# Skip term and gate product as single VectorE steps, with Q ahead of V and a new order of all steps, in an attention and Mamba-2 kernel on one core

## The chip, the cores and the metric

The kernel runs on one core of one Trainium2 chip. The metric is the device time of one execution in microseconds; where several executions were made, their median. A core has five engines that run side by side and wait for each other by semaphores: PE (TensorE, matmuls into PSUM), DVE (VectorE), ACT (ScalarE), POOL (GpSimd) and SP (SyncE, which here only issues DMAs).

## What is computed

The input x is 4 images of 128 channels and 32 x 32 points, so 1024 tokens of 128 channels for each of 4 batches. A block of attention is followed by a Mamba-2 block. Cut to what matters:

```python
# attention, per batch
h = group_norm(x, 8 groups) * gn_w + gn_b
q, k, v = split(h @ qkv_w.T + qkv_b)
x = (softmax(q @ k.T / sqrt(128)) @ v) @ proj_w.T + proj_b + x

# Mamba-2, per batch, on tokens of x
u = layernorm(x) * norm_g + norm_b
z, xBC, dt = split(u @ in_w.T)
dt = softplus(dt + dt_bias)
xs, Bm, Cm = split(silu(conv4(xBC) + conv_b))        # causal, 4 taps, one filter per channel
state_t = state_{t-1} * exp(dt_t * A) + dt_t * xs_t * Bm_t
y = state_t . Cm_t + Dp * xs                          # Dp * xs is the skip term
y = y * silu(z)                                       # the gate product
y = y * rsqrt(mean(y*y) + eps) * rms_w
out = y @ out_w.T
pooled = mean(out over tokens)
attn = sigmoid(relu(pooled @ se1_w.T + se1_b) @ se2_w.T + se2_b)
result = x + out * attn
```

## The kernel before

**Batches and steps.** The four batches are called a, b, c and d. The work of all of them is cut into named steps, and one table, `ORDER` (lines 59 to 130), lists every step once: the name of its kind, a number, the batch, and for some the PSUM bank (`@0` to `@2`). Each engine walks through the whole table and emits the steps that are its own, so the table alone sets the order of the instructions on every engine; semaphore waits hold each step until what it needs is there. Attention of one batch is laid over the Mamba block of the batch before it.

**Attention.** `h` (float32), `h_hi` and `h_lo` are the normalised input and its split in two halves of lower precision. `Q0`, `Q1` multiply them with the product of the key and query weights, ACT makes `q_hi` and DVE `q_lo`. `V0`, `V1` are the values (line 1093). For each of 8 tiles of 128 queries there are two halves of keys: `S` (the scores, three matmuls of 512 columns each, line 1103), `max` on DVE over both halves (line 879), two `exp` on ACT (line 597), two transposes `T` on PE (line 1111), their copies `pT` on ACT (line 603) and two `PV` on PE (line 1120). So `S0` and `S1` are the first tile and `S14`, `S15` the last. Then DVE scales and adds (`inv`, `res`) and takes the statistics of the layer norm (`stats`, `ln_ve`).

**Mamba, in halves of 512 tokens.** `UT` transposes the normalised tokens, `InX`, `InBC`, `InZ` and `Dt` project them. `conv_x` are four taps: the first on ACT, the others on DVE (line 918). `conv_bc` has its taps on ACT (`term`, line 636) and POOL (line 508). `sp0` to `sp17` are the softplus on DVE. `L0` to `L7` are matmuls that spread decays to the chunks of 128 tokens, and `l` the DVE scans over them (line 969); `m` (line 981) multiplies them with `G`. `to_end` (DVE), `xend` (POOL), `U` (PE), `st` (a scan on DVE, line 989), `stc` (ACT) and `Yo` (PE) carry the state from chunk to chunk; `Y` is the part inside a chunk.

**What the change touches.** `yo` on DVE (line 998) brings in the state's part. The skip term is two steps on POOL: `dx` (lines 524 and 526) is `xs * Dp`, held in the buffer of `sq`, and `yo_dx` (line 532) adds it. `y` on DVE (line 1005) adds the chunk's part. The gate product is made of `zt`, the tanh of z/2, and `zv`, z/2, both on ACT, and two POOL steps per half: one multiplies, one adds (line 501). `g` (line 536 on POOL, line 1014 on DVE for the last half of batch d) applies it. `sq`, `Ss`, `ms`, `y_pow` give the inverse root in `y_rstd`; `Out` is the output projection, `o` (line 707) its scaled copy, `Pl` (line 1241) the sums over tokens, `pl`, `SeA`, `hdn`, `SeB`, `tha` the small network behind them, `gated` (line 1022) and `fin` the last two operations, and a DMA carries each half out.

**The start.** The attention weights come by three DMAs on one semaphore, `attn_w_in`: `wqkv`, `wpT` and `ob_row`. `kq_mm` and `vp_mm` on PE wait for all three. `gn_stats0`, `gn_mm10`, `gn_dev0`, `gn_mm20`, `gn_ve0`, `gn_pow0`, `gn_aff0` are the group norm's steps of batch a, and `warm` are matmuls whose result is not used.

## Time and profile before

| what | value |
|---|---|
| median of 3 runs | 313.5 us (313.08 to 313.89) |
| the profiled execution | 313.5 us |
| its span, first to last instruction | 311.8 us |
| mean granted TensorE clock | 0.977 |
| PE busy | 277.1 us, 89% |
| DVE busy | 238.7 us, 77% |
| ACT busy | 205.6 us, 66% |
| POOL busy | 139.5 us, 45% |

The span is the time of the profiled execution without 1.7 us around it. The profile says for each engine how long it was busy and, for each stretch of idle time, whose work ended it. A wait costs time only where the waiting engine is the one that sets the end of its stretch. Matmuls are pipelined and their rows overlap, so the sum of their durations is more than the busy time.

### The profile page before, as it was taken

How to read it: one execution, taken by the hardware profiler on the slowest of the kernel's cores; microseconds unless marked ns; L12 is line 12 of the kernel's file. 1: busy time of each engine (PE TensorE's matmuls, PEld its weight loads, DVE VectorE, ACT ScalarE, POOL GpSimd, SP SyncE). 2: the span in 40 equal slices, each digit the busy share in tenths (PEclk: the TensorE clock that was granted, in tenths of full speed). 3: DMA queues.
4: the chain of work that ended last, by engine and by line, in shares of the span. 5: the costliest groups of instructions: out<-in, count | busy, mean ns of one | idle time of the engine just before them, and what ended most of it. 6: DMA issues, size and time to landing. Idle time of an engine off the chain costs nothing.

```text
span 311.8 us, 6225 instructions
## 1 busy us (share of the span) xinstructions
PE 277.1 (89%) x2016; PEld 231.5 (74%) x2016; DVE 238.7 (77%) x520; ACT 205.6 (66%) x401; POOL 139.5 (45%) x146
## 2 busy tenths in 40 slices
PE   2689999999999999999999999997999997869762
PEld 1677898887678988878897888786789875637661
DVE  5657555596989759677997999798886898988823
ACT  1134578887796875898759748867857856684230
POOL 7110102521139401853482512990627285775980
PEclk9999999999999999999999999999999999995995
DMA  6900000000000000000000000100000000000003
GB/s 182 408 29 1 2 0 3 0 2 0 2 0 2 3 2 0 0 2 3 1 2 0 2 0 2 38 34 0 2 0 2 2 2 1 0 2 0 37 34 135
DMA packets 3786, 7.32 MB, mean 23 GB/s; under 512 B 651, under 2 KB 1580, under 8 KB 3756
## 3 DMA queue, kind: packets, MB, share of 16 engines
q1 hardware_dynamic: 3212, 6.72, 5.8%
q8 instruction: 17, 0.28, 0.4%
q10 hardware_dynamic: 544, 0.21, 0.2%
q14 instruction: 13, 0.11, 0.1%
HBM read 4.83 MB, written 2.10 MB: 22 GB/s over the span
## 4 chain that ended last, share of the span: by engine, by line
PE 56%; DVE 18%; issue 10%; POOL 7%; ACT 6%; DMA 2%; DVEq 0%; SPq 0%; ACTq 0%; POOLq 0%
PE mamba L1039 18%; PE scores L1039 14%; PE attn_out L1039 14%; PE turn L1111 6%; DVE neg_max L879 3%; PE turn L1039 2%; DVE L L969 2%; DMA ob_row<-in_proj_b 2%; POOL gate L501 2%; ACT probs L597 1%; DVE pre L918 1%; POOL ln_rstd L490 1%; DVE x_all L1022 1%; POOL y_rstd L541 1%; DVE ln_raw L894 1%
## 5 line engine op out<-in xcount | busy, mean ns | idle before, releaser
L1039 PE MATMUL attn_out<-values,pT 128*128 128x129 f32 x512 | 67.3, 276 | 2.3 <-DVE res L890 1.8
L1039 PEld LDWEIGHTS attn_out<-values,pT 128*128 128x128 f32 x512 | 62.7, 191 | 8.4 <-issue 7.1
L597 ACT ACTIVATE probs<-scores,neg_max 128x512 f32<-128x512 f32 x64 | 41.8, 683 | 14.7 <-DVE neg_max L879 13.8
L879 DVE TENSOR_REDUCE neg_max<-scores 128x1 f32<-128x1024 f32 x32 | 39.0, 1218 | 15.4 <-PE scores L1039 15.4
L603 ACT ACTIVATE pT<-turn 128x512 f32<-128x512 f32 x64 | 37.7, 593 | 13.7 <-PE turn L1111 12.1
L969 DVE TENSOR_TENSOR_SCAN L<-mamba,ident 128x512 f32<-128x512 f32 x32 | 38.6, 1215 | 4.8 <-PE mamba L1039 4.6
L1111 PE MATMUL turn<-ident,probs 128*128 128x128 f32 x256 | 38.2, 274 | 0.0
L1111 PEld LDWEIGHTS turn<-ident,probs 128*128 128x128 f32 x256 | 30.7, 143 | 5.1 <-issue 2.0
L508 POOL TENSOR_TENSOR pre<-pre,th 128x512 f32<-128x512 f32 x16 | 21.7, 1353 | 27.0 <-issue 13.0
L1039 PE MATMUL scores<-h_hi,q_hi 128*128 128x512 f32 x64 | 29.3, 457 | 3.6 <-ACT probs L597 2.3
L1039 PE MATMUL mamba<-u,winC 128*128 128x512 f32 x48 | 25.1, 607 | 0.8 <-DVE L L981 0.5
L1039 PE MATMUL scores<-h_hi,q_lo 128*128 128x512 f32 x64 | 25.3, 395 | 0.0
L1039 PE MATMUL scores<-h_lo,q_hi 128*128 128x512 f32 x64 | 25.1, 393 | 0.0
L515 POOL TENSOR_TENSOR xend<-xdt,to_end 128x512 f32<-128x512 f32 x8 | 9.5, 1192 | 34.7 <-DVE to_end L976 17.1
L501 POOL TENSOR_TENSOR gate<-gate,zv 128x512 f32<-128x512 f32 x16 | 20.9, 1306 | 8.9 <-ACT gate L654 8.6
L490 POOL TENSOR_TENSOR ln_rstd<-ln_var,neg_half 128x4 f32<-128x4 f32 x8 | 9.4, 1175 | 33.6 <-DVE ln_var L901 33.5
L981 DVE TENSOR_TENSOR L<-L,mamba 128x512 f32<-128x512 f32 x32 | 20.9, 676 | 2.3 <-PE mamba L1039 2.2
L918 DVE SCALAR_TENSOR_TENSOR pre<-raw,vec,pre 128x512 f32<-128x512 f32 x24 | 19.1, 794 | 1.1 <-ACT pre L629 1.0
L1039 PEld LDWEIGHTS scores<-h_hi,q_hi 128*128 128x128 f32 x64 | 12.1, 189 | 8.6 <-issue 5.8
L1039 PE MATMUL mamba<-dA_head,pick_chunk 128*128 128x512 f32 x32 | 15.9, 512 | 0.7 <-DVE y L1005 0.3
L610 ACT ACTIVATE u_tok<-res,ln_rstd 128x128 f32<-128x128 f32 x32 | 10.2, 394 | 6.9 <-POOL ln_rstd L490 6.9
L697 ACT ACTIVATE stateT<-scanned 128x512 f32<-128x512 f32 x8 | 9.1, 1144 | 8.5 <-DVE scanned L989 8.5
(198 smaller groups left out, 626.2 us busy)
## 6 DMA issues: line engine op xcount, KB each, us to landing
res<-in_x_tok SPq DMA_DIRECT2D x4, 512.0 KB, 7.8
out<-res SPq DMA_DIRECT2D x8, 256.0 KB, 2.0
x_all<-in_x SPq DMA_DIRECT2D x3, 512.0 KB, 8.3
x_all<-in_x SPq DMA_DIRECT2D x2, 256.0 KB, 3.2
winT<-in_in_wT SPq DMA_DIRECT2D x1, 194.0 KB, 6.7
wqkv<-in_qkv_w ACTq DMA_DIRECT2D x1, 192.0 KB, 3.6
wpT<-in_proj_wT SPq DMA_DIRECT2D x1, 64.0 KB, 3.6
ob_row<-in_proj_b SPq DMA_DIRECT2D x1, 64.0 KB, 5.9
```

Of the source, the lines that this page charges most:

```text
L490: pool.tensor_tensor(ln_rstd[:, four], ln_var[:, four], neg_half[:, four], ALU.pow).then_inc(ln_rstd_ready.sem, 1)
L501: pool.tensor_tensor(gate[:, half], gate[:, half], zv[:, half], ALU.add if part else ALU.mult).then_inc(gate_ready.sem, 1)
L508: pool.tensor_tensor(pre[:, 1, half_of(n)], pre[:, 1, half_of(n)], term(b, n, j), ALU.add).then_inc(tap["bc"].sem, 1)
L597: act.activation(probs[:, i % 2, half_of(h)], scores[:, half_of(h)], ACT.Exp, bias=neg_max[:, i:i + 1]).then_inc(exp_done.sem, 1)
L603: act.activation(pT[:, i % 2, QUAD * h:QUAD * (h + 1), :], bank[:, :].rearrange("p (a b) -> p a b", a=QUAD), ACT.Copy).then_inc(pT_ready.s ...
L610: last = act.activation(u_tok[:, i, :], res[:, b, i, :], ACT.Copy, scale=ln_rstd[:, i:i + 1])
L879: V.tensor_reduce(neg_max[:, n:n + 1], scores[:, :], AX.X, ALU.max, negate=True).then_inc(max_ready.sem, 1)
L918: V.scalar_tensor_tensor(pre[:, 0, half_of(n)], raw[:, 0, n * HALF + j:(n + 1) * HALF + j], vec[:, CONV_X + j:CONV_X + j + 1], pre[:, 0, h ...
L969: V.tensor_tensor_scan(L[:, HEADS * n:HEADS * (n + 1), :].rearrange("p a b -> p (a b)"), bank[:, :], ident4[:, :, :].rearrange("p a b -> p ...
L981: V.tensor_tensor(M[:, HEADS * n:HEADS * (n + 1), :], L[:, HEADS * n:HEADS * (n + 1), :], bank[:, tile(c)].unsqueeze(1).broadcast_to([P, H ...
L1039: return T.matmul(o, w, v, start=start, stop=stop)
L1111: last = T.transpose(bank[:, tile(c)], probs[:, i % 2, tile(QUAD * h + c)], ident[:, :])
```

## The change

- **Skip term.** `dx` is gone. `yo_dx` is one DVE instruction, `(xs * Dp) + yo`; for the first half a second, small one writes the first chunk of 128 tokens.
- **Gate product.** One DVE instruction per half, `(gate + 1) * zv`, in place of the two on POOL.
- **Convolution, first half of batch d alone.** Its three later x taps go from DVE to ACT (`term_x`) and POOL.
- **Start.** The weights have two semaphores, so `kq_mm` waits for `wqkv` alone. `gn_mm10` stands ahead of `kq_mm`, `V0` and `V1` behind `Q0` and `Q1`, `vp_ev` behind `Q0`, and there are 5 warm matmuls in place of 10.
- **Last sums, batch d.** `Out` is copied unscaled (`o_raw`), and `Pl` multiplies the unscaled copy with `y_rstd` as its moving column, so `Pl` no longer waits for `o`. `o` scales from that copy into the buffer of `gated`.
- **Order.** The table is written anew throughout. Of the 32 tiles of scores (8 in each batch) 18 now have their two score steps next to each other on PE, in place of 15; the others have one or more steps between them.

```diff
 ORDER = """
-gn_stats0 warm3 kq_mm gn_mm10 vp_mm gn_dev0 kq_ev gn_mm20 gn_ve0 vp_ev gn_pow0 gn_aff0 h0a h_hi0a V0a@0 h_hi1a h_lo0a
-h1a warm10 Q0a h_lo1a q_hi0a win_s Q1a v0a V1a@1 gn_bs3 v1a q_hi1a q_lo0a q_lo1a S0a gn_bs1 S1a win_mm max0a xob0a
...
+gn_stats0 warm3 gn_mm10 kq_mm gn_dev0 gn_mm20 kq_ev vp_mm gn_ve0 gn_pow0 gn_aff0 h0a h_hi0a h_hi1a h_lo0a h1a warm5
+Q0a vp_ev h_lo1a q_hi0a Q1a q_lo0a V0a@1 win_s q_hi1a q_lo1a S0a S1a gn_bs3 win_mm max0a V1a@0 gn_bs2 exp0a v0a S2a
...
@@ signals and helpers
-        dx = sq
-        vec_in, attn_w_in = signal("vec_in"), signal("attn_w_in")
+        vec_in, qkv_w_in, proj_w_in = signal("vec_in"), signal("qkv_w_in"), signal("proj_w_in")
+        def x_on_pool(b, n):
+            return (b, n) == (BATCH - 1, 0)
+        def term_x(n, j):
+            return th[:, 0, half_of(n)] if j % 2 else x_all[:, half_of(n)]
@@ POOL
-                elif kind == "gate":
...
-                    pool.tensor_tensor(gate[:, half], gate[:, half], zv[:, half], ALU.add if part else ALU.mult
-                                       ).then_inc(gate_ready.sem, 1)
+                elif kind == "conv_x" and n % TAPS and x_on_pool(b, n // TAPS):
...
+                    pool.tensor_tensor(pre[:, 0, half_of(n)], pre[:, 0, half_of(n)], term_x(n, j), ALU.add
+                                       ).then_inc(tap_x_pool.sem, 1)
-                elif kind == "dx":
...
-                        pool.tensor_scalar(yo[:, 0:P], xs[:, 0:P], vec[:, DP:DP + 1], 0.0, ALU.mult, ALU.add)
...
-                    pool.tensor_scalar(dx[:, part], xs[:, part], vec[:, DP:DP + 1], 0.0, ALU.mult, ALU.add
-                                       ).then_inc(dx_ready.sem, 1)
-                elif kind == "yo_dx":
...
-                    pool.tensor_tensor(yo[:, part], yo[:, part], dx[:, part], ALU.add).then_inc(yo_dx_ready.sem, 1)
@@ ACT
+                elif kind == "term_x":
...
+                    act.activation(term_x(n, j), raw[:, 0, n * HALF + j:(n + 1) * HALF + j], ACT.Copy,
+                                   scale=vec[:, CONV_X + j:CONV_X + j + 1]).then_inc(term_x_ready.sem, 1)
+                elif kind == "o_raw":
+
+                    bank = take(act, b, "Out", n)
+                    act.activation(o_tok[:, QUAD * n:QUAD * (n + 1), :], bank[:, :].rearrange("p (i c) -> p i c", i=QUAD),
+                                   ACT.Copy).then_inc(o_raw_ready.sem, 1)
@@ DVE
+                elif kind == "yo_dx":
+
+                    part = slice(P, HALF) if n == 0 else half
+                    if n == 0:
+                        V.tensor_scalar(yo[:, 0:P], xs[:, 0:P], vec[:, DP:DP + 1], None, ALU.mult)
+                    wait(dve, yo_ready, b, n + 1)
+                    V.scalar_tensor_tensor(yo[:, part], xs[:, part], vec[:, DP:DP + 1], yo[:, part], ALU.mult, ALU.add
+                                           ).then_inc(yo_dx_ready.sem, 1)
+                elif kind == "gate":
+
+                    wait(dve, zt_ready, b, n + 1)
+                    wait(dve, zv_ready, b, n + 1)
+                    V.scalar_tensor_tensor(gate[:, half], gate[:, half], 1.0, zv[:, half], ALU.add, ALU.mult
+                                           ).then_inc(gate_ready.sem, 1)
@@ PE
-                        wait(pe, o_ready, b, n + 1)
+                        wait(pe, o_raw_ready, 0, n + 1)
+                        wait(pe, y_rstd_ready, b, n + 1)
                         tiles = [o_tok[:, QUAD * n + k, :] for k in range(QUAD)]
                     for k, t in enumerate(tiles):
-                        last = mm(bank[:, 0:1], t, ones[:, 0:1], k == 0, k == len(tiles) - 1)
+                        factor = ones[:, 0:1] if b < BATCH - 1 else y_rstd[:, QUAD * n + k:QUAD * n + k + 1]
+                        last = mm(bank[:, 0:1], t, factor, k == 0, k == len(tiles) - 1)
```

Three places show the new order on an engine. In the rows, `scores<-ident` are the warm matmuls, `key_query` belongs to Q, `value_proj` to V, `turn<-ident,probs` is T and `attn_out` is PV.

The first is the start on PE, from its first matmul. Before:

```order
L1039 MATMUL scores<-ident 128x128 x3
L1039 MATMUL turn<-wqkv 128x128
L1039 MATMUL turn<-vec,wqkv 128x1
L1039 MATMUL mamba<-gn_mv,group_avg 128x1
L1039 MATMUL turn<-wpT,wqkv 128x128
L1039 MATMUL turn<-wpT,vec 128x128
L1039 MATMUL mamba<-gn_dev,group_avg 128x1
L1039 MATMUL turn<-value_proj,h 128x128 x4
L1039 MATMUL scores<-ident 128x128 x10
L1039 MATMUL scores<-h_hi,key_query_hi 128x512
```

And now:

```order
L1075 MATMUL scores<-ident 128x128 x3
L1075 MATMUL mamba<-gn_mv,group_avg 128x1
L1075 MATMUL turn<-wqkv 128x128
L1075 MATMUL turn<-vec,wqkv 128x1
L1075 MATMUL mamba<-gn_dev,group_avg 128x1
L1075 MATMUL turn<-wpT,wqkv 128x128
L1075 MATMUL turn<-wpT,vec 128x128
L1075 MATMUL scores<-ident 128x128 x5
L1075 MATMUL scores<-h_hi,key_query_hi 128x512
L1075 MATMUL scores<-h_lo,key_query_hi 128x512
L1075 MATMUL scores<-h_hi,key_query_lo 128x512
L1075 MATMUL scores<-h_hi,key_query_hi 128x512
```

The group norm's first matmul has moved ahead of the one that waits for weights, and V0 from ahead of Q to behind it.

The second is PE from the very last scores of batch d (S15) on. Here `xend,BT` is U, `pick_chunk` is L, `ident,xs` is XsT, `BC,stateT` is Yo and `u_tok` is UT. Before:

```order
L1039 MATMUL scores<-h_hi,q_lo 128x512
L1039 MATMUL attn_out<-values,pT 128x129 x4
L1039 MATMUL mamba<-winC,u 128x128 x4
L1111 MATMUL turn<-ident,probs 128x128 x8
L1039 MATMUL mamba<-u,winC 128x512
L1039 MATMUL mamba<-ones,o_sum 128x1 x2
```

And now:

```order
L1075 MATMUL scores<-h_hi,q_lo 128x512
L1148 MATMUL turn<-ident,probs 128x128 x4
L1075 MATMUL mamba<-xend,BT 128x128 x4
L1075 MATMUL attn_out<-values,pT 128x129 x4
L1075 MATMUL mamba<-dA_head,pick_chunk 128x512
L1207 MATMUL mamba<-ident,xs 128x128 x4
L1075 MATMUL attn_out<-values,pT 128x129 x8
L1075 MATMUL mamba<-BC,stateT 128x128 x3
L1075 MATMUL mamba<-dA_head,pick_chunk 128x512
L1148 MATMUL turn<-ident,probs 128x128 x4
L1075 MATMUL attn_out<-values,pT 128x129 x8
L1148 MATMUL turn<-ident,probs 128x128 x4
```

U0, L6, Yo0 and L7 of batch c stood ahead of the last scores and now stand behind them, and nine PV steps of batch d are left there in place of seven.

The third is DVE near its end, from `to_end1` of batch d on. Before:

```order
L976 COPY to_end<-L 128x16
L1022 SCALAR_TENSOR_TENSOR x_all<-th_att,y 128x512
L998 TENSOR_TENSOR th<-mamba,decay_in 128x384
L981 TENSOR_TENSOR L<-L,mamba 128x512 x2
L989 SCALAR_TENSOR_TENSOR scanned<-chunk_decay,mamba 128x512
L1005 TENSOR_TENSOR y<-mamba,th 128x512
L981 TENSOR_TENSOR L<-L,mamba 128x512 x2
L998 TENSOR_TENSOR th<-mamba,decay_in 128x512
L1022 SCALAR_TENSOR_TENSOR x_all<-th_att,y 128x512
L1005 TENSOR_TENSOR y<-mamba,th 128x512
```

And now:

```order
L997 COPY to_end<-L 128x16
L1053 COPY pooled<-mamba 128x1
L1033 SCALAR_TENSOR_TENSOR gate<-gate,zv 128x512
L1002 TENSOR_TENSOR L<-L,mamba 128x512 x3
L1010 SCALAR_TENSOR_TENSOR scanned<-chunk_decay,mamba 128x512
L1058 SCALAR_TENSOR_TENSOR x_all<-th_att,y 128x512
L1002 TENSOR_TENSOR L<-L,mamba 128x512
L1040 TENSOR_TENSOR y<-mamba,th 128x512
L1058 SCALAR_TENSOR_TENSOR x_all<-th_att,y 128x512
L1019 TENSOR_TENSOR th<-mamba,decay_in 128x512
L1027 SCALAR_TENSOR_TENSOR th<-xs,vec,th 128x512
L1040 TENSOR_TENSOR y<-mamba,th 128x512
```

The last gate product and the last skip term have come onto DVE, and the first half's `yo` has moved ahead of this stretch.

## Rows read from the trace of the kernel before

**Rows 1.** Busy time by stage: stretch, length, busy time of each engine, PE clock, DMA.

```profile
0.00:21.10 21.10, 12.23 (x61) 11.39 (x61) 12.56 (x39) 4.25 (x7) 7.34 (x31) 1.00 0.64 229
21.10:237.00 215.90, 207.80 (x1503) 175.34 (x1504) 169.15 (x372) 162.00 (x311) 86.35 (x76) 1.00 0.01 4
237.00:255.20 18.20, 17.86 (x156) 15.15 (x154) 17.04 (x38) 13.02 (x29) 9.75 (x9) 1.00 0.01 3
255.20:288.00 32.80, 26.23 (x160) 18.50 (x158) 28.76 (x53) 20.95 (x44) 21.53 (x20) 0.90 0.00 1
288.00:297.90 9.90, 6.60 (x96) 5.50 (x96) 7.47 (x13) 1.93 (x3) 8.28 (x7) 1.00 0.08 29
297.90:311.80 13.90, 6.41 (x46) 5.56 (x46) 3.76 (x10) 3.44 (x11) 6.25 (x5) 0.73 0.24 94
```

**Rows 2.** Timeline of PE, start to second tile: start, length, instruction, [idle before].

```profile
4.82 1.65 PE L1039 MATMUL scores<-ident 128*128 128x128 f32 x6 [4.82 <-POOL sp_coef L459]
8.11 0.80 PE L1039 MATMUL turn<-wqkv 128*128 128x128 f32 x2 [1.64 <-DMA ob_row<-in_proj_b]
...
8.98 0.57 PE L1039 MATMUL mamba<-gn_mv,group_avg 128*128 128x1 f32 x2
...
13.31 2.04 PE L1039 MATMUL turn<-value_proj,h 128*128 128x128 f32 x8 [2.34 <-DVE h L866]
15.14 3.56 PE L1039 MATMUL scores<-ident 128*128 128x128 f32 x20
18.46 0.48 PE L1039 MATMUL scores<-h_hi,key_query_hi 128*128 128x512 f32 x1
...
19.93 1.05 PE L1039 MATMUL turn<-value_proj,h 128*128 128x128 f32 x8
21.06 0.47 PE L1039 MATMUL scores<-h_hi,q_hi 128*128 128x512 f32 x1
...
26.19 0.47 PE L1039 MATMUL scores<-h_hi,q_hi 128*128 128x512 f32 x1 [0.69 <-ACT probs L597]
```

**Rows 3.** Timeline of DVE, the same stretch, columns as above.

```profile
6.19 0.21 DVE L798 BATCH_NORM_AGGREGATE gn_mv<-gn_raw 128x2 f32<-128x12 f32 x1
...
12.62 0.55 DVE L866 TENSOR_SCALAR h<-x_all,gn_scale,gn_bias 128x512 f32<-128x512 f32 x1
13.53 0.69 DVE L871 TENSOR_TENSOR h_lo<-h,h_hi 128x512 fp32r<-128x512 f32 x1 [0.37 <-ACT h_hi L580]
```

**Rows 4.** The page's part 6, DMA issues: size and time to landing.

```profile
wqkv<-in_qkv_w ACTq DMA_DIRECT2D x1, 192.0 KB, 3.6
```

**Rows 5.** Groups of instructions by shape: busy time, mean ns, idle time before them.

```profile
L969 DVE TENSOR_TENSOR_SCAN L<-mamba,ident 128x512 f32<-128x512 f32 x32 | 38.6, 1215 | 4.8 <-PE mamba L1039 4.6
...
L981 DVE TENSOR_TENSOR L<-L,mamba 128x512 f32<-128x512 f32 x32 | 20.9, 676 | 2.3 <-PE mamba L1039 2.2
L501 POOL TENSOR_TENSOR gate<-gate,zv 128x512 f32<-128x512 f32 x16 | 20.9, 1306 | 8.9 <-ACT gate L654 8.6
L918 DVE SCALAR_TENSOR_TENSOR pre<-raw,vec,pre 128x512 f32<-128x512 f32 x24 | 19.1, 794 | 1.1 <-ACT pre L629 1.0
...
L532 POOL TENSOR_TENSOR th<-th,sq 128x512 f32<-128x512 f32 x4 | 5.4, 1356 | 0.7 <-DVE th L998 0.6
```

**Rows 6.** Line 1022 on DVE: durations ns, least, median, most.

```profile
L1022 DVE SCALAR_TENSOR_TENSOR x_all<-th_att,y x8: 681/688/1759, 186.6 to 307.4; 128x512 f32<-128x512 f32 x8
```

**Rows 7.** Waits of DVE from 237 to 298: us in total, times, longest.

```profile
DVE y L1005 <- POOL th L532: 1.2, 1, 1.2
```

**Rows 8.** Timeline of POOL near the end, columns as in rows 2.

```profile
295.62 1.58 POOL L532 TENSOR_TENSOR th<-th,sq 128x512 f32<-128x512 f32 x1 [0.62 <-DVE th L998]
...
300.88 1.02 POOL L541 TENSOR_TENSOR y_rstd<-ms,neg_half 128x4 f32<-128x4 f32 x1
```

**Rows 9.** Timeline of ACT, then of PE, near the end.

```profile
302.14 1.14 ACT L707 ACTIVATE y<-mamba,y_rstd 128x128 f32<-128x128 f32 x4 [1.37 <-PE mamba L1039]
...
303.43 1.03 PE L1039 MATMUL mamba<-ones,y 128*128 128x1 f32 x8 [0.59 <-ACT y L707]
```

221 lines of the change are left out of this document (118 added, 103 removed).

## The prediction

> **What bounds the kernel now.** I read the busy time by stage first [rows 1]. The stages are cut at the first scores of batch a (21.1 us), the last scores of batch d (237.0), the last PV (255.2), the end of the last scan over L (288.0) and the last `y` (297.9). From 21.1 to 237.0 PE is busy for 207.8 of 215.9 us: this is a PE stretch, with 8.1 us of idle time in all, and DVE works there for 169.2. From 237.0 to 297.9 DVE is busy for 17.04 + 28.76 + 7.47 = 53.3 of 60.9 us, and PE for 50.7: DVE sets the pace, and its idle time is 7.6 us. Behind 297.9 and ahead of 21.1 nothing is full: both ends are chains, in which each engine waits for another. POOL, from which the change takes most work, is busy for 86 of the 216 us in the PE stretch and is the bound of no stage.
>
> So the change has four places to act: the chain at the start, the PE work between the first and the last scores, the DVE work behind the last scores, and the chain at the end.
>
> **The start.** The group norm's first matmul has its input at 6.40 [rows 3] and PE has ended the three warm steps at 6.47, but it stands behind `kq_mm`, which waits for the third weight until 8.11, and so runs at 8.98 [rows 2]. Put ahead, it runs at 6.5, which is 2.5 earlier. `kq_mm` now stands between it and the second one, and its own weight needs only 3.6 us to land [rows 4], so it costs that chain some 0.1. `h` comes at 10.2 in place of 12.62. Q0 needs `h_lo`, done at 13.53 + 0.69 = 14.22 [rows 3], now at 11.8; before, it had to wait for V0 (2.04) and ten warm steps (3.56) as well and ran at 18.46 [rows 2]. Five warm steps take half of 3.56 and end near 11.6, behind the two weight products. So Q0 starts at 11.9, 6.6 earlier. Not all of it stays: Q1 now waits for the second `h_lo`, which on DVE comes behind the second `h` (0.55 as the first [rows 3]) and `vp_ev` (two small ones, some 0.6) and takes 0.69, so Q1 starts near 13.6. It takes 0.7 (both Q ran from 18.46 to 19.93), and V0 (1.05) still stands ahead of the first scores, which start near 15.5 in place of 21.06 [rows 2]. The second tile's scores follow 5.1 behind the first's now (26.19), and as the steps between are nearly the same, the gain there is 5.4 to 5.7. One thing can take from it. V0's eight matmuls took 2.04 us at 13.31, and V1's eight took 1.05 at 19.93, behind the warm steps [rows 2]: the same work at half the pace, which are TensorE's levels of 1.2 and 2.4 GHz. PE had been at work from 13.31 on before it grew faster. If the clock is still at the lower level through Q, V0 and the first scores, V0 costs 1.0 more and the six to nine matmuls of 512 columns on the path some 0.2 each, in all 2.2 to 2.8. The start is worth 3.0 to 5.7. I take 5.0, nearer to the upper end, since PE is now at work with few breaks from 6.5 on.
>
> **The PE stretch.** Taking POOL work away gives nothing here, because PE does not wait for it. What counts is which PE steps lie between the first and the last scores. Two PV of batch d (8 instructions each as the rows count them), U0 (8), Yo0 (6), G1 (8) and L6, L7 (1 each) of batch c and UT0 of batch d (4) have moved behind the last scores: 44. V0 of batch a (8), and Pl1, SeA, SeB of batch b (4, 4, 2) have moved in: 18. At 207.8 / 1503 = 0.138 us each, net 26 instructions are 3.6 us less [rows 1]. I take 3.5. The pairs of scores are no term: most tiles have them nearly adjacent already, and the sum of PE's work is the same.
>
> **DVE behind the last scores.** This is what the other moves are paid with. Onto DVE behind the last scores come, by the new table:
> - moved from ahead: the scans of L5, L6, L7 of batch c, 3 x 1.215 = 3.6; `st0`, also a scan of 512, 1.2; `m0` to `m4`, 5 x 0.676 = 3.4 [rows 5]; `inv`, `res`, `stats` of tile 3, `ln_ve0`, `yo0`, `to_end1`, nine instructions of 128 columns or less and one of 384, an estimate of 2.1 together;
> - new on DVE: three gate products and four skip terms. The trace has no such instruction; the nearest is the tap, with the same form and both inputs in SBUF, 0.794 in the mean [rows 5], and the least for such a form is 0.681 [rows 6]. I take 0.74 each, 5.2, and 0.4 for two small ones.
> - gone: the three taps of batch d, 3 x 0.794 = 2.4; `xs1` of batch c, 0.7, and both `gated` of batch b, which stood here and took 1.7 each [rows 6], 3.4; and two copies of one column, 0.3.
>
> The sum is 3.6 + 1.2 + 3.4 + 2.1 + 5.6 - 2.4 - 4.1 - 0.3 = 9.1 us more, or 62.4 in place of 53.3. In the other stages the new DVE steps lie under PE: there DVE has 46.8 us idle in 216, and five gate products and four skip terms need 6.6. If DVE's idle time of 7.6 stays, the stretch is 70.0 and costs 9.1; if it halves, 66.2 and 5.3. Some of it must go, because DVE has more work in store while it waits, and because one wait falls away: `y` waited 1.2 for POOL's skip add [rows 7], which took 1.58 [rows 8]. I take 5.0 idle, so 67.4, and 6.5 us more. The three taps now go through ACT and POOL, which have 35.9 and 39.6 busy in these 60.9 us, so they are hidden; without that cover they cost POOL's 3 x 1.356, the price of such an addition [rows 5], in a row.
>
> **The end.** `y_pow` is ready at 301.90 [rows 8], but the sums Pl1 start at 303.43, behind `o` (302.14 to 303.28) [rows 9]. Now Pl1 needs the factor and an unscaled copy by one instruction in place of `o`'s four, which took 1.14 [rows 9]. The copy begins as `o` did, when the output product is there; if it takes half, 0.57, Pl1 starts near 302.8. The gain is between 0.4 and 1.1; I take 0.8, above that half, since `o` of the first half is out of its way too.
>
> **Sum.** The profiled execution took 313.5, its span 311.8 and 1.7 around it, and it equals the median. 313.5 - 5.0 - 3.5 + 6.5 - 0.8 = 310.7.
>
> **A rule against it.** Both `gated` of batch b took 1.7 us, two and a half times their median of 0.688, while POOL was at its additions; the most is 1.759 [rows 6]. The Trainium skill, page "SBUF — State Buffer", section "Who interferes with whom", says that a VectorE instruction with two SBUF inputs and a GpSimd instruction that reads SBUF share a port by an exclusive lock, so that the later one waits until the other is through. The trace agrees in so far as the median is near the least and the most is 1.08 us above it. By that rule the new DVE steps are of the kind that gets held up, and the removed POOL steps are of the kind that holds up.
>
> **Rivals.**
> 1. *DVE is the bound behind the last scores and the new steps are held up (slower).* For: DVE was already at 88% there, and two of eight `gated` took 1.7. Against: POOL has 8 us less to do in the same stretch. If the seven new ones take 0.5 more each (half of 1.759 - 0.74), 3.5, and the idle time stays at 7.6: -5.0 - 3.5 + 9.1 + 3.5 - 0.8 = +3.3, so 316.8. It decides from the point where that stretch grows by more than 9.3 us. This is the port's rule at work, too.
> 2. *The terms cancel.* DVE keeps its idle time, since its waits are for PE and ACT and not for lack of work, and nothing is held up: -5.0 - 3.5 + 9.1 - 0.8 = -0.2, so 313.3. The low clock through the first steps comes to the same with a shorter tail: -3.0 - 3.5 + 6.5 - 0.8 = -0.8.
> 3. *A much larger gain.* The start keeps 5.7, DVE's idle time falls to 3.0, and with POOL's fewer steps some 2 us of held-up time leave DVE: 9.1 - 4.6 - 2.0 = +2.5; -5.7 - 3.5 + 2.5 - 0.8 = -7.5, so 306.0.
>
> **How the numbers follow.** A measurement here tells 0.3%, 0.9 us, from no change: faster is under 312.6, slower over 314.4. The forecast (308.8 to 312.6) has 0.41, rival 3 (below 308.8) 0.24, rival 2 (to 314.4) 0.17, rival 1 (above) 0.18. Faster 0.65, same 0.17, slower 0.18. The range goes from 305.0, under rival 3's time, to 316.5, with about 0.1 left out on each side.
>
> **What would show it.** The first scores should start between 15.4 and 18.5. From first to last scores it should take 211 to 214 us with PE busy for all but 8. Behind the last scores DVE should be busy for about 62 us until the last `y`, in a stretch of 66 to 70. The new DVE steps should take 0.69 to 0.8; a share of them near 1.7 speaks for rival 1. The last `Pl` should start right after the factor or the copy, and not after `o`. I am wrong if the PE stretch itself is not shorter, because then the order has waits on PE that the counting of steps does not see, or if the last stretch is set by a chain through POOL and PE and not by DVE's load.

## The result, and the profile after

The changed kernel takes 303.3 us (median of 4, 301.26 to 304.12), where the kernel before takes 313.7 (median of 4, 313.08 to 314.19) beside it: a ratio of 0.966, with a 95% interval of 0.960 to 0.972. Timed again with the last experiments it took 303.9 beside 313.9 (0.967, 0.964 to 0.970). The forecast was 310.7, the range 305.0 to 316.5: the sign was right, the gain was 10.4 us in place of 2.8, and the time lies 1.7 us under the range.

The profiled execution took 301.26 us, span 299.2 and 2.0 around it. These are its stages, cut at the same events as [rows 1], with the same columns (length, busy time of PE, PE's weight loads, DVE, ACT, POOL, granted clock, DMA):

```profile
0.00:15.50 15.50, 10.55 (x43) 9.07 (x43) 10.17 (x37) 4.33 (x6) 6.06 (x30) 1.00 0.83 298
15.50:225.00 209.50, 202.67 (x1481) 171.55 (x1480) 174.00 (x370) 159.60 (x311) 64.14 (x54) 1.00 0.01 2
225.00:245.80 20.80, 19.56 (x152) 17.49 (x151) 19.68 (x49) 11.57 (x24) 4.94 (x5) 1.00 0.07 27
245.80:277.40 31.60, 24.67 (x188) 16.66 (x187) 30.30 (x60) 24.98 (x50) 19.97 (x17) 1.00 0.01 1
277.40:287.00 9.60, 7.57 (x109) 6.48 (x109) 8.97 (x15) 2.32 (x4) 5.48 (x4) 1.00 0.15 56
287.00:299.20 12.20, 5.41 (x46) 4.85 (x44) 3.83 (x9) 4.80 (x13) 4.47 (x4) 0.80 0.23 87
```

Beside [rows 1], by stage:

| stage | before | after | difference | forecast |
|---|---|---|---|---|
| to the first scores | 21.1 | 15.5 | -5.6 | -5.0 |
| first to last scores | 215.9 | 209.5 | -6.4 | -3.5 |
| last scores to last `y` | 60.9 | 62.0 | +1.1 | +6.5 |
| behind the last `y` | 13.9 | 12.2 | -1.7 | -0.8 |

The four differences add up to -12.6 us and not to the -10.4 of the medians, because the profiled execution was the shortest of all. A profile of the repeated one, 302.6 us, has 14.9, 211.2, 62.2 and 12.3 in these stages: -6.2, -4.7, +1.3 and -1.6.

From here on the second stage is called the PE stretch, the third the tail. In the tail DVE is now busy for 58.95 us (53.27 before) and idle for 3.05 (7.6 before).

The start on PE, as [rows 2]:

```profile
6.46 0.59 PE L1075 MATMUL mamba<-gn_mv,group_avg 128*128 128x1 f32 x2
...
11.88 0.77 PE L1075 MATMUL scores<-h_hi,key_query_hi 128*128 128x512 f32 x1
...
14.66 1.05 PE L1075 MATMUL turn<-value_proj,h 128*128 128x128 f32 x8
15.47 0.48 PE L1075 MATMUL scores<-h_hi,q_hi 128*128 128x512 f32 x1
```

The group norm's first product runs at 6.46 (forecast 6.5), Q at 11.88 (11.9), the first scores at 15.47 (near 15.5). Q0's first matmul takes 0.77 against 0.48 in [rows 2], which is the pace of the lower level; V0 at 14.66 takes 1.05, so PE was at full pace by then. This is read from the durations alone: the granted clock in the profile's row for this stretch is 1.00.

The new and the moved DVE steps, as groups by shape (as [rows 5]: busy time, mean ns, idle before):

```profile
L939 DVE SCALAR_TENSOR_TENSOR pre<-raw,vec,pre 128x512 f32<-128x512 f32 x21 | 15.5, 740 | 0.2
L1033 DVE SCALAR_TENSOR_TENSOR gate<-gate,zv 128x512 f32<-128x512 f32 x8 | 5.5, 684 | 0.1
L1058 DVE SCALAR_TENSOR_TENSOR x_all<-th_att,y 128x512 f32<-128x512 f32 x6 | 4.0, 678 | 0.0
L1027 DVE SCALAR_TENSOR_TENSOR th<-xs,vec,th 128x512 f32<-128x512 f32 x4 | 4.0, 993 | 0.0
L1027 DVE SCALAR_TENSOR_TENSOR th<-xs,vec,th 128x384 f32<-128x384 f32 x4 | 3.5, 871 | 0.0
```

The gate product (L1033) takes 0.684 and is never held up. The skip term (L1027) runs from 0.614 to 1.677: two of its eight are held up. `gated` (L1058) had a most of 1.759 in [rows 6]; none is long now. The tap (L939) fell from 0.794 to 0.740 in the mean.

The end, ACT, POOL and PE, as [rows 8, 9]:

```profile
290.58 0.60 ACT L716 ACTIVATE y<-mamba 128x512 f32<-128x512 f32 x1
...
289.93 1.01 POOL L542 TENSOR_TENSOR y_rstd<-ms,neg_half 128x4 f32<-128x4 f32 x1 [0.81 <-DVE ms L1043]
...
290.38 1.92 PE L1075 MATMUL mamba<-y_rstd,y 128*128 128x1 f32 x16
```

The factor of the second half is done at 290.94 and the unscaled copy (290.58) takes 0.60 in place of 1.14; both sums run as one row from 290.38 on, no longer behind `o`.

### The profile page after: what moved, and what is told of

Its sections match the earlier page's. It is cut to its first block, busy times and chain, and to the rows that moved or that the text cites. A ratio compares the mean times of both kernels' runs of the same rounds, so it can differ in the third digit from the quotient of the medians.

```text
span 299.2 us, 6186 instructions
## 1 busy us (share of the span) xinstructions
PE 270.4 (90%) x2006; PEld 226.1 (76%) x2006; DVE 247.0 (83%) x537; ACT 207.6 (69%) x406; POOL 105.1 (35%) x113
## 4 chain that ended last, share of the span: by engine, by line
PE 66%; DVE 17%; issue 8%; ACT 5%; POOL 3%; DVEq 0%; ACTq 0%; POOLq 0%
PE mamba L1075 20%; PE scores L1075 17%; PE attn_out L1075 15%; PE turn L1148 7%; PE turn L1075 3%; DVE L L990 2%; DVE neg_max L900 2%; DVE th L1027 1%; DVE sp_sum L795 1%; POOL pre L524 1%; PE mamba L1166 1%; PE mamba L1207 1%; DVE L L1002 1%; DVE scanned L1010 1%; DVE res L911 1%
## 5 line engine op out<-in xcount | busy, mean ns | idle before, releaser
L1075 PE MATMUL attn_out<-values,pT 128*128 128x129 f32 x512 | 65.8, 276 | 2.5 <-DVE res L911 2.4
L1075 PEld LDWEIGHTS attn_out<-values,pT 128*128 128x128 f32 x512 | 62.2, 191 | 7.3 <-issue 4.9
L598 ACT ACTIVATE probs<-scores,neg_max 128x512 f32<-128x512 f32 x64 | 42.9, 686 | 24.6 <-DVE neg_max L900 22.2
L524 POOL TENSOR_TENSOR pre<-pre,th 128x512 f32<-128x512 f32 x16 | 20.7, 1292 | 27.6 <-ACT pre L630 22.2
L1002 DVE TENSOR_TENSOR L<-L,mamba 128x512 f32<-128x512 f32 x32 | 21.1, 675 | 0.4 <-PE mamba L1075 0.4
L510 POOL TENSOR_TENSOR ln_rstd<-ln_var,neg_half 128x4 f32<-128x4 f32 x8 | 8.5, 1063 | 31.3 <-DVE ln_var L922 31.1
L939 DVE SCALAR_TENSOR_TENSOR pre<-raw,vec,pre 128x512 f32<-128x512 f32 x21 | 15.5, 740 | 0.2
L542 POOL TENSOR_TENSOR y_rstd<-ms,neg_half 128x4 f32<-128x4 f32 x8 | 8.9, 1113 | 18.6 <-DVE ms L1043 18.6
L504 POOL TENSOR_TENSOR h_lo<-h,h_hi 128x512 fp32r<-128x512 f32 x6 | 7.5, 1277 | 22.4 <-ACT h_hi L581 22.4
L537 POOL TENSOR_TENSOR xs<-y,gate 128x512 f32<-128x512 f32 x7 | 9.3, 1335 | 17.2 <-DVE y L1040 17.2
```

Of the source, the lines that this page charges most:

```text
L524: pool.tensor_tensor(pre[:, 1, half_of(n)], pre[:, 1, half_of(n)], term(b, n, j), ALU.add).then_inc(tap["bc"].sem, 1)
L537: pool.tensor_tensor(y2[:, half], y[:, half], gate[:, half], ALU.mult).then_inc(y2_ready.sem, 1)
L542: pool.tensor_tensor(y_rstd[:, four], ms[:, four], neg_half[:, four], ALU.pow).then_inc(y_rstd_ready.sem, 1)
L598: act.activation(probs[:, i % 2, half_of(h)], scores[:, half_of(h)], ACT.Exp, bias=neg_max[:, i:i + 1]).then_inc(exp_done.sem, 1)
L939: V.scalar_tensor_tensor(pre[:, 0, half_of(n)], raw[:, 0, n * HALF + j:(n + 1) * HALF + j], vec[:, CONV_X + j:CONV_X + j + 1], pre[:, 0, h ...
L1002: V.tensor_tensor(M[:, HEADS * n:HEADS * (n + 1), :], L[:, HEADS * n:HEADS * (n + 1), :], bank[:, tile(c)].unsqueeze(1).broadcast_to([P, H ...
```

## The experiments

Each ran beside the kernel before on the same chip; its median there was 313.9 to 314.0. "Held-up time" is a sum over DVE's instructions: what each takes over the shortest one of its shape, where that is more than 0.1 us. In the tail it is 7.0 us in the kernel before and 2.9 in the changed one. In the PE stretch it went the other way, from 8.7 to 12.4, so the whole kernel has 16.0 before and 15.6 after: in the changed kernel the held-up time has moved from where DVE sets the pace to where PE does.

### Each part alone

In diffs of the table only the steps that change stand, with their neighbours.

The start, in the old order:

```diff
-gn_stats0 warm3 kq_mm gn_mm10
+gn_stats0 warm3 gn_mm10 kq_mm
...
-h_hi0a V0a@0
...
-warm10 Q0a
+warm5 Q0a vp_ev
...
-Q1a v0a V1a@1
+Q1a q_lo0a V0a@0
...
+max0a V1a@1
...
-                    pe.wait_ge(attn_w_in.sem, 48)
+                    pe.wait_ge(qkv_w_in.sem, 16)
```

> The kernel before with the new start alone: two weight semaphores, the group norm's first matmul ahead of the weight product, V0 and V1 behind Q0 and Q1, five warm matmuls. All else stands in the old order. Theory A (a gain at the head is passed on in full, since PE is full behind it): the first scores start near 15.5 in place of 21.1 and the time falls by 5.0 to 5.6 us, to about 308.3. Rival B (the gain is eaten, since V0 and V1 now fall behind the first scores on an engine that is full, or since the first steps run at the lower clock level): the first scores start near 15.5 too, but the stretch from first to last scores grows by 1.5 us or more, and the time is 310 or more.

Measured: 307.9 us, ratio 0.981 (0.978 to 0.983), so -6.1. First scores at 14.9, PE stretch 215.5 (215.9 before). Theory A: the head's gain is passed on in full.

The end, in the old order:

```diff
-y_pow0d sq1d fin1b o0d
+y_pow0d sq1d o_raw0d fin1b o0d
...
-fin0c o1d pl0d
+o_raw1d fin0c o1d pl0d
...
-                        last = mm(bank[:, 0:1], t, ones[:, 0:1], k == 0, k == len(tiles) - 1)
+                        last = mm(bank[:, 0:1], t, y_rstd[:, QUAD * n + k:QUAD * n + k + 1],
+                                  k == 0, k == len(tiles) - 1)
```

> The kernel before with the new end alone: the output product of batch d is copied unscaled, and the last sums take the factor as moving column. Theory A: the last sums start behind the factor in place of behind the scaled copy, 0.8 to 1.7 us earlier, and the time is 312.0 to 312.8. Rival B (the copy by one instruction takes as long as the four, so the sums wait for it instead): 313.4 to 313.7, no change.

Measured: 312.6, ratio 0.995 (0.993 to 0.997), -1.4. The part behind the last `y` went from 13.9 to 13.0. Theory A.

The move alone, in the old order; `gate0` and `gate1` are now DVE's two, at the place of each half's first POOL step, and `yo_dx` is DVE's at its old place:

```diff
-dx0a xs1a pT8b T9b@1 gate1a PV5b
+xs1a pT8b T9b@1 PV5b
...
-dx1a term1b
+term1b
...
-max3c gate2a
+max3c gate1a
...
-PV3c gate3a L1b@1
+PV3c L1b@1
...
```

> The kernel before in its old order and with its old start and end, but gate product and skip term are one DVE instruction each; the two POOL steps of each are gone. Seven of the sixteen new instructions of 512 columns lie behind the last scores. Theory A (load decides): DVE has 7 x 0.69 + 0.3 = 5.1 us more there, the wait of 1.2 for POOL falls away, so the time rises by about 3.9 to 317.5. Theory B (POOL's reading additions hold DVE's instructions up, and their going frees it): of 7.0 us of held-up DVE time in that stretch some 4 go, so the time is 313.0 to 314.5, and the held-up part is near 3 us. Theory C (both, and DVE's steps were waiting for POOL in more places than the profile names): under 312.5.

Measured: 315.0, ratio 1.005 (1.002 to 1.008), +0.9. This is the run that corrects the forecast. The tail took 60.7 us (60.9 before) with all seven new steps in it: DVE's busy time rose by only 0.3 us, because held-up time fell from 7.0 to 2.8, as theory B had it (the time is 0.5 over its range). In the whole kernel held-up time fell from 16.0 to 10.7. What was lost was lost in the PE stretch (217.5 in place of 215.9), where one such place reads, DVE, POOL, PE:

```profile
125.46 1.20 DVE L754 SCALAR_TENSOR_TENSOR dt<-dtx,sp_log 128x16 f32<-128x16 f32 x1
...
125.36 1.27 POOL L477 TENSOR_TENSOR res<-res,ob_row 128x512 f32<-128x512 f32 x1
...
127.77 0.40 PE L1026 MATMUL mamba<-la,upto 128*128 128x16 f32 x2 [1.16 <-DVE la L758]
```

With the skip term gone from POOL's queue another POOL addition came 2.3 us earlier and met `dt`, sixteen columns, which took 1.20 us where it took 0.18 before; PE stood for 1.16; in the kernel before it came to the same matmul 1.05 earlier (126.72). So the move takes held-up time away in one place and can put it on PE's path in another.

The order alone: the changed kernel with the POOL steps put back. `dx` stands ahead of each `yo`, `yo_dx` where it stood, and each `gate` is two POOL steps in a row:

```diff
-yo0d
+dx0d yo0d
...
+                    pool.tensor_tensor(gate[:, half], gate[:, half], zv[:, half], ALU.mult).then_inc(gate_step.sem, 1)
+                    wait(pool, gate_step, b, n + 1)
+                    pool.tensor_tensor(gate[:, half], gate[:, half], zv[:, half], ALU.add).then_inc(gate_ready.sem, 1)
-                    V.scalar_tensor_tensor(gate[:, half], gate[:, half], 1.0, zv[:, half], ALU.add, ALU.mult
-                                           ).then_inc(gate_ready.sem, 1)
```

> The changed kernel with its new start, end and order, but gate product and skip term are again two POOL steps each (the skip term's first right ahead of the state's part, its second in the new place). Theory A (load decides): DVE has 5.1 us less behind the last scores, so the time falls below that of the changed kernel, to some 299. Theory B (POOL's additions hold DVE up and are waited for): the held-up DVE time in that stretch rises from 2.9 to about 7 us and waits for POOL come back, so the time is 302 to 306, above the changed kernel's 303.3 or level with it. Rival C (in the new order the POOL steps stand on the path): 306 or more. Either way, what is left to 313.6 is what start, order and end give without the move.

Measured: 314.1, ratio 1.001 (0.998 to 1.004): none of the start's 6.1 and the end's 1.4 is left. With DVE having 11 us less to do in all, the tail took 69.8 us, and the PE stretch 214.7. Theory A is wrong, and theory B's 302 to 306 is missed too: it is rival C, 306 or more. It was also run with the three x taps of batch d back on DVE, so that every engine's load is that of the kernel before:

> The changed kernel's start, end and order with gate product and skip term back on POOL, and the three x taps of batch d's first half back on DVE as well, so that no engine's load differs from the kernel before. Theory (the order was written for POOL with less work, and the three taps in POOL's queue are what crowd it behind the last scores): the stretch from the last scores to the last y falls from 69.8 us to 64 to 67 and the time from 314.1 to 309 to 312. Rival (the stall is spread over gate and skip steps alike): 313 or more.

Measured: 313.0, ratio 0.998 (0.995 to 1.000), tail 70.1, as its rival said: the taps aren't it.

### Old and new order, with and without the move

> All parts of the change but the new table of the middle: new start, new end, gate product and skip term as single DVE steps, in the old order from the first scores on. Theory (the parts add up): 314.0 - 6.1 (start, measured) - 1.4 (end, measured) + 0.9 (moves, measured) = 307.4, and the new order gives the 4.1 us that are left to the changed kernel. Rival (the start's gain frees the moves or the order from a wait): 305 or less.

> New start and new end in the old order, gate product and skip term still on POOL. If start and end add up: 314.0 - 6.1 - 1.4 = 306.5. With that, the four combinations of old or new order with POOL or DVE steps are complete: old/POOL 306.5, old/DVE 307.4, new/POOL 313.0 (measured), new/DVE 303.3 (measured). Rival (the two ends share a gain): 307.5 or more.

Measured: 308.8 (0.983, 0.981 to 0.985), 1.4 over the sum of parts that was expected, and 306.2 (0.975, 0.973 to 0.977). All four have the new start and end. In the table stands the time, and behind it the tail with DVE's idle time in it, from the profiles:

| | steps on POOL | steps on DVE |
|---|---|---|
| old order | 306.2; 61.4, idle 8.1 | 308.8; 61.7, idle 6.8 |
| new order | 313.0 to 314.1; 69.8 to 70.1, idle 11.9 to 12.2 | 303.3 to 303.9; 62.0 to 62.2, idle 3.1 to 3.3 |

Start and end add up to 306.2 (306.5 expected). From there the move alone costs 2.6, the order alone 7 to 8, and both together gain 2.6 (306.2 to 303.6, the middle of the two timings). The terms do not add: a table of the order is good or bad only together with what stands on POOL. DVE's idle time shows the same: neither the order nor the move alone brings it down to 3. Why the move costs 2.6 behind the new start and 0.9 behind the old one was not followed up; in the profiles PE again waits 1.1 us for `la` there.

### Why the new order cannot bear the POOL steps

Two mechanisms can be read off the traces. First, held-up instructions in the PE stretch. The order-only kernel, DVE, POOL, PE:

```profile
114.80 1.24 DVE L962 SCALAR_TENSOR_TENSOR pre<-raw,vec,pre 128x512 f32<-128x512 f32 x1
...
116.22 1.52 DVE L962 SCALAR_TENSOR_TENSOR pre<-raw,vec,pre 128x512 f32<-128x512 f32 x1
...
114.22 1.27 POOL L539 TENSOR_TENSOR gate<-gate,zv 128x512 f32<-128x512 f32 x1
115.56 1.63 POOL L541 TENSOR_TENSOR gate<-gate,zv 128x512 f32<-128x512 f32 x1
...
120.85 0.47 PE L1084 MATMUL scores<-h_hi,q_hi 128*128 128x512 f32 x1 [1.32 <-ACT probs L621]
```

And the changed kernel at the same place:

```profile
114.86 0.74 DVE L939 SCALAR_TENSOR_TENSOR pre<-raw,vec,pre 128x512 f32<-128x512 f32 x1
...
115.78 0.68 DVE L1033 SCALAR_TENSOR_TENSOR gate<-gate,zv 128x512 f32<-128x512 f32 x1
116.38 0.74 DVE L939 SCALAR_TENSOR_TENSOR pre<-raw,vec,pre 128x512 f32<-128x512 f32 x1
...
120.23 0.47 PE L1075 MATMUL scores<-h_hi,q_hi 128*128 128x512 f32 x1 [0.85 <-ACT probs L598]
```

Beside the two POOL steps the two taps take 0.50 and 0.78 longer; that is more than the 0.68 that the gate product costs on DVE. DVE does one instruction more and is done earlier, and PE stands for 0.85 in place of 1.32. Over the whole stretch held-up time is 16.1 us against 12.4, and the stretch is 214.7 against 209.5 and 211.2.

Second, POOL's queue in the tail. The order-only kernel near the end of batch d, POOL, PE, DVE:

```profile
285.45 1.26 POOL L539 TENSOR_TENSOR gate<-gate,zv 128x512 f32<-128x512 f32 x1
286.79 1.26 POOL L541 TENSOR_TENSOR gate<-gate,zv 128x512 f32<-128x512 f32 x1
288.02 1.05 POOL L533 TENSOR_TENSOR xend<-xdt,to_end 128x512 f32<-128x512 f32 x1
...
289.49 1.49 PE L1084 MATMUL mamba<-xend,BT 128*128 128x128 f32 x6
...
291.11 1.22 DVE L1033 TENSOR_TENSOR_SCAN scanned<-chunk_decay,mamba 128x512 f32<-128x512 f32 x1 [1.91 <-PE mamba L1084]
...
294.08 2.08 PE L1084 MATMUL mamba<-BC,stateT 128*128 128x128 f32 x8
```

The changed kernel:

```profile
278.16 1.44 POOL L531 TENSOR_TENSOR xend<-xdt,to_end 128x512 f32<-128x512 f32 x1 [1.11 <-DVE xdt L983]
...
280.00 0.83 PE L1075 MATMUL mamba<-xend,BT 128*128 128x128 f32 x6
...
280.96 1.22 DVE L1010 TENSOR_TENSOR_SCAN scanned<-chunk_decay,mamba 128x512 f32<-128x512 f32 x1 [0.21 <-PE mamba L1075]
...
283.43 1.16 PE L1075 MATMUL mamba<-BC,stateT 128*128 128x128 f32 x8 [0.59 <-ACT stateT L708]
```

Nobody needs the gate product soon, but it stands ahead of `xend` in the new table (the old one had its second POOL step behind it). So `xend`, then U, then DVE's scan wait for it: the scan waits 1.91 in place of 0.21. And PE, having stood, does the same products at the lower clock (granted 0.86 from 288 to 290 and 0.50 from 290 to 296, where the changed kernel has 1.00 throughout): U 1.49 in place of 0.83, Yo 2.08 in place of 1.16.

That it is the place in POOL's queue, and not the gate product itself, a run of the next section shows. It is the changed kernel with fills at the places of these steps, which read nothing and for which nobody waits. POOL, then DVE:

```profile
281.74 2.85 POOL L496 MEMSET fill_b<- 128x512 f32 x5
284.67 1.05 POOL L541 TENSOR_TENSOR xend<-xdt,to_end 128x512 f32<-128x512 f32 x1
...
288.00 1.22 DVE L1020 TENSOR_TENSOR_SCAN scanned<-chunk_decay,mamba 128x512 f32<-128x512 f32 x1 [2.49 <-PE mamba L1085]
```

The fills stand ahead of `xend`, and the scan waits 2.49.

Which of the two moved operations it is:

> The changed kernel with the gate product alone back on POOL as two steps (16 additions or products of 1.3 us there); the skip term stays on DVE. Theory H (held-up DVE instructions and a later POOL cost, whoever waits for the result): 306 to 309, with y not waiting for a skip term. Theory W (what costs is y's wait for the skip term on POOL): under 304.

> The changed kernel with the skip term alone back on POOL as two steps (12 of 1.3 us and four of 0.4 us there); the gate product stays on DVE. Theory H: 306 to 309, about the same as with the gate product, since POOL's extra work is about the same. Theory W: 311 to 314, nearly all of what both cost together.

Measured: gate product alone back on POOL, ratio 0.988 (0.984 to 0.991), about 310.2 us; skip term alone, 306.6 (0.977, 0.974 to 0.980). The first is the loosest figure of this document: its twelve executions lie between 307.7 and 313.6 with a median of 312.1, and the ratio leaves the longest five out. Neither expectation fits in full. The skip term, on which `y` waits (2.3 us for POOL in that run), costs 2.7 to 3, as theory H had it; the gate product, on which nobody waits, costs about 6.5 (8.4 by the median of all twelve), more than twice as much and more than H said. Theory W is wrong. In the profile with the gate product on POOL (an execution of 313.2) the tail is 69.3, the scan waits 1.9 again, and the PE stretch is 214.8; with the skip term on POOL they are 63.7 and 211.1, and 2.4 us more are lost behind the last `y`, at a granted clock of 0.60.

### POOL's additions, without any use

Both are the changed kernel with more on POOL. Additions:

```diff
+                if kind in ("gate", "yo_dx"):
+                    for _ in range(2):
+                        pool.tensor_tensor(fill_b[:, :], ident4[:, :, :].rearrange("p a b -> p (a b)"), fill_b[:, :], ALU.add).then_inc(fill_step.sem, 1)
+                        filled_n[0] += 1
+                        pool.wait_ge(fill_step.sem, filled_n[0])
```

Fills:

```diff
+                if kind in ("gate", "yo_dx"):
+                    for _ in range(5):
+                        pool.memset(fill_b[:, :], 0.0).then_inc(fill_step.sem, 1)
+                        filled_n[0] += 1
+                        pool.wait_ge(fill_step.sem, filled_n[0])
```

> The changed kernel, and on POOL at each of the sixteen places of a gate product or skip term two extra additions of 512 columns that read SBUF twice and that nobody waits for (2 x 1.3 us, 41.7 us in all). DVE, ACT and PE have exactly the changed kernel's work. Theory B (a reading POOL addition holds DVE instructions up, and through them PE): the held-up DVE time grows by 5 us or more, the granted clock has dips in the PE stretch, and the time is 306 to 314. Rival (what costs is that POOL's other work comes later, behind the extra one): the same rise as with extra fills of the same length. Theory A (only waits for the gate product and the skip term counted, and these are gone): under 304.

> As the run with extra additions, but with five fills of 512 columns at each of the sixteen places (5 x 0.52 us, the same 41.6 us in all), which write SBUF and read nothing. Theory B: the held-up DVE time stays near the changed kernel's, and the time is the changed kernel's plus what POOL's lateness costs, 303 to 306, clearly under the run with additions. Rival (POOL's lateness alone): equal to the run with additions.

Measured: with additions 317.7 (1.014, 1.010 to 1.017), with fills 308.8 (0.985, 0.982 to 0.987); both are over the ranges expected (306 to 314, 303 to 306). POOL's busy time is nearly alike (150.3 and 146.1 us). DVE's is not: 259.5 and 248.0, for the same instructions, with 29.1 and 18.7 us of held-up time. The groups by shape, first with additions, then with fills:

```profile
L1043 DVE SCALAR_TENSOR_TENSOR gate<-gate,zv 128x512 f32<-128x512 f32 x8 | 7.4, 926 | 0.0
L1037 DVE SCALAR_TENSOR_TENSOR th<-xs,vec,th 128x512 f32<-128x512 f32 x4 | 4.8, 1188 | 0.0
L1012 DVE TENSOR_TENSOR L<-L,mamba 128x512 f32<-128x512 f32 x32 | 21.1, 674 | 0.5 <-PE mamba L1085 0.5
```

```profile
L1043 DVE SCALAR_TENSOR_TENSOR gate<-gate,zv 128x512 f32<-128x512 f32 x8 | 5.5, 685 | 0.1
L1037 DVE SCALAR_TENSOR_TENSOR th<-xs,vec,th 128x512 f32<-128x512 f32 x4 | 3.0, 742 | 0.0
L1012 DVE TENSOR_TENSOR L<-L,mamba 128x512 f32<-128x512 f32 x32 | 21.1, 676 | 0.6 <-PE mamba L1085 0.6
```

The steps with both inputs in SBUF take 926 and 1188 ns beside POOL's additions, 685 and 742 beside its fills; `m`, with one input in PSUM, takes 674 and 676. So of the 14 us that the additions cost, about 5 are POOL's lateness (the fills cost that too, all of it in the tail: 69.1 us), and 9 come from POOL's reading and what it sets off, lower clock included. The Trainium skill, page "SBUF — State Buffer", section "Who interferes with whom", says just this: two SBUF inputs on VectorE collide with a GpSimd instruction that reads SBUF, and not with one that only writes it. The runs agree.

### DVE's load in the tail

Ahead of each of the seven steps there, in the changed kernel:

```diff
+                    if b == BATCH - 1 or (b == BATCH - 2 and (kind, n) != ("gate", 0)):
+                        ones4 = ident4[:, :, :].rearrange("p a b -> p (a b)")
+                        V.scalar_tensor_tensor(fill_b[:, :], ones4, 1.0, ones4, ALU.add, ALU.mult)
```

> The changed kernel with one extra DVE instruction of 512 columns (0.68 us, two SBUF inputs, result unused) at each of the seven places of a gate product or skip term behind the last scores, 4.8 us in all. Theory A (DVE's load sets that stretch, as the forecast assumed): the stretch and the time grow by 4 to 5 us, to 307 to 308.5. Rival (the chain through PE, ACT and POOL sets it as well, so part of the load fits into idle time): under 306.5, with DVE's idle time of 3.05 us reduced.

Measured: 311.8, ratio 0.992 (0.989 to 0.995), 8.2 over the changed kernel's 303.6. Both expectations are missed: the load costs more than itself. Its tail:

```profile
225.90:247.30 21.40, 19.56 (x151) 17.51 (x151) 20.28 (x50) 11.54 (x24) 5.29 (x5) 1.00 0.07 26
247.30:284.30 37.00, 27.22 (x190) 18.88 (x188) 34.74 (x64) 25.27 (x50) 20.69 (x17) 0.91 0.01 1
284.30:295.80 11.50, 9.48 (x112) 8.18 (x111) 10.12 (x18) 2.31 (x4) 6.08 (x4) 0.85 0.12 47
```

69.9 us in place of 62.0. DVE is busy for 65.1 (+6.2: 4.8 of load and 2.0 more of held-up time, from 2.9 to 4.9, less some overlap), and its idle time did not fill but rose from 3.05 to 4.8.

The opposite, less load, with the skip term of three halves made by PE:

```diff
+                            if (b, n) in SKIP_ON_PE:
+                                mm(to, dp_diag[:, h * HEADDIM:(h + 1) * HEADDIM], xs[:, tile(QUAD * n + c)], True, False)
-                            last = mm(to, xdt[:, r, :], M[:, r, :])
+                            last = mm(to, xdt[:, r, :], M[:, r, :], (b, n) not in SKIP_ON_PE)
```

> The changed kernel, with the skip term of both halves of batch c and the first of batch d made by PE: ahead of each of Y's products one more with a diagonal of Dp, summed in the same bank, so that three DVE steps of 384 or 512 columns (0.61, 1.68 held up, 0.61 us in the changed kernel) fall away, and PE has 16 more products per half, some 0.5 to 1.1 us each. Theory A (behind the last scores DVE's load counts, and PE has 5 us or more to spare): 1.5 to 2.9 us less, 300.5 to 301.8. Rival (PE is as near to the bound there, or y waits for the longer Y): 303 or more.

Measured: 303.7, ratio 0.967 (0.964 to 0.970), no change: the rival. DVE is busy for 3.0 us less in the tail and idle for 4.5 more; PE is busier and its clock falls to 0.95 and 0.85. (The profiled execution is the longest of its six, 305.8, with a tail of 63.5.) The taps of batch d back on DVE:

> The changed kernel with the three x taps of batch d's first half back on DVE (0.74 each), in place of ACT and POOL. Theory A (behind the last scores DVE's load counts): 2.2 us more on DVE there, the time rises by 1 to 2.2 us. Theory B (what POOL reads out of SBUF is what counts): POOL loses three additions of 1.3 there, and with them some of 2.9 us of held-up DVE time, so the time rises by less than 1 us or falls.

Measured: 303.6, ratio 0.967 (0.964 to 0.970), no change, though DVE has 1.0 us more busy time in the tail. That fits theory B; but the executions spread from 301.8 to 305.3 and the profiled tail is 63.0, so one microsecond either way isn't excluded.

### The clock behind PE's gaps

The clock fell in the tail of most kernels and not in that of the profiled changed one (it did in the repeated one: 0.95 in the middle part). Twenty-six dummy matmul steps were put into PE's gaps there:

```diff
-Cum1d@2
+warm3 Cum1d@2
...
-DAT1d@2
+warm2 DAT1d@2
...
-XsT1d@1
+warm2 XsT1d@1
...
-U1d@2
+warm2 U1d@2
...
```

> The changed kernel itself, timed on the same chip as the three beside it: 303.3 as before, between 301 and 304.5.

> The changed kernel with 26 dummy matmul steps on PE behind the last PV of batch d (products of the identity into the idle score bank, one to three in a place), put into PE's gaps there; they compute nothing that is used and wait for nothing. Theory C (the clock falls behind PE's gaps and that costs): those executions whose mean clock is 0.975 to 0.98 are the ones that lose, so the median falls by 0.5 to 2 us, to 301.3 to 302.8. Rival (dummies cost PE time and the clock is of no weight there): 303.5 to 306.

> The kernel with 4.8 us of extra DVE load (311.8), with the same dummy matmuls. Theory C (3.7 of its 8.5 us of loss is the clock, which falls to 0.91 and 0.85 behind the last PV): the clock stays near 1.00 there, PE is busy with dummies, and the time falls to 308 to 309.5. Rival (the loss over 4.8 us is something else, a wait of DVE for a chain): 311.5 or more, at whatever clock.

> The new order with gate product and skip term on POOL (314.1), with the same dummy matmuls. Theory C: the clock there was 0.95 and 0.75, so the time falls by 1.5 to 3 us, to 311 to 312.5. Rival (waits for POOL alone make the stretch long): 314 or more.

Measured: 303.9; with dummies **302.2 (0.962, 0.960 to 0.965)**; the kernel with extra load 311.8 to 309.5; the order-only kernel 314.1 to 313.0. All three gain, by 1.7, 2.3 and 1.1. The changed kernel with dummies is the fastest version found by its median, though the two intervals just touch; its five executions lie between 302.20 and 302.30, those of the changed kernel beside it between 302.41 and 304.29. The order-only kernel's 313.0 lies between its theory (311 to 312.5) and its rival (314 or more). Its tail has the full clock:

```profile
246.80:278.40 31.60, 28.23 (x222) 21.05 (x220) 30.01 (x60) 25.04 (x50) 19.89 (x17) 1.00 0.00 1
278.40:288.00 9.60, 9.24 (x118) 7.83 (x118) 8.96 (x15) 2.34 (x4) 5.49 (x4) 1.00 0.15 56
```

For the order-only kernel the tail went from 69.8 to 68.2 at a clock of 1.00, so the clock is 1.6 us of the 7.8 that it lost there; the rest is left to the waits. In the profiles of the kernel with extra load the tail shrank by 0.7 only, and its clock was still 0.95 in the middle part. But these two are not alike: the one without dummies is the shortest of its nine executions (310.0), the one with them among the longest of its six (311.1), with 1.4 us more in the PE stretch. The other part of the 2.3 is not located.

## Why the prediction was right and wrong

**The start** was right in mechanism, and 0.6 to 1.1 us low in size: 15.47 for "near 15.5", and -5.6 in the profile, -6.1 alone (forecast -5.0). The lower pace that it allowed for reached Q only.

**The PE stretch** was right in kind and low in size: -3.5 forecast, -6.4 and -4.7 in the two profiles. Steps did leave it, and its idle time fell from 8.1 to 6.8 and 6.9, which the counting left out. The price of a step was low: at the same granted clock, 1.00, PE is busy for 202.67 us in place of 207.80, 5.1 less and not 3.6. In the repeated execution it is 204.30, just 3.5 less, but at a clock of 0.99, so that it meets the term exactly is luck. (What moved in is V1, not V0 as the text says there; the count is the same.)

**DVE behind the last scores** is the term that failed: +6.5 forecast, +1.1 measured (+1.3 in the repeated execution). Its load was counted well: by the shortest duration of each instruction the tail has 11.4 us more, and the forecast's items at such prices come to about 11. The miss of 5.4 us is in what was made of the load, 62.4 busy and 5.0 idle where 58.95 and 3.05 came.

- *Held-up time, 1.7 to 2.0 us.* The sum took the new steps at 0.74 and left the old ones at their old durations. But held-up time in the tail fell from 7.0 to 2.9 us. The sum had 2.1 of these 4.1, in the two `gated` that it took out at 1.7 each; the others that came free (two `xs` at up to 1.72, `to_end`, two steps of the softplus) it did not see. The move in the old order shows it alone (7.0 to 2.8, tail 60.7 with 5 us more work), and the additions without use show the cause (9 us between reading and filling). The text had the rule, had its row [rows 6], and used it against the change only; rival 3 had the right sign and, with 2.0 on top of the two `gated`, the right size.
- *Overlap of rows, 1.8 us.* The sum added durations to a busy time. DVE's rows overlap by some 0.05 us each as they follow one another, and with 122 in place of 102 of them the durations in the tail exceed the busy time by 6.4 in place of 4.7: they grew by 7.4, the busy time by 5.7.
- *The idle time, 2.0 us.* 7.6 was taken to fall to 5.0 because DVE "has more work in store". It fell to 3.05, and not for that reason: more load in store made it rise to 4.8. In the table of four it is near 3 only with the new order and the steps off POOL together, and 12 with the new order and the steps on POOL, where DVE waits for U and Yo behind a late `xend`. Which waits of the old order the new one takes away was not isolated.

The forecast priced the change stage by stage and never asked whether order and move bear on each other. Alone, each costs time (7 to 8 and 2.6); together they gain 2.6.

**The end** was right in mechanism and low in size: -0.8 forecast, -1.4 alone, -1.7 in the profile. The sums started by the factor, and both halves ran back to back.

**The rivals.** The new steps held up (1): two of sixteen, 2 us. Nothing of it in the gate products. The much larger gain (3) was the right one with its two causes: its start of 5.7, its idle time of 3.0 and its held-up time of 2.0 all came true. It was priced at 306.0 and still came out high, by 1.2 to 2.9 us in the PE stretch, 0.9 at the end and 1.4 in the tail, most of it the overlap. The range stopped at 305.0, 1 us under rival 3's own time, although none of these terms had been given a bound on that side.
